# The images stage of a fused attention and expert kernel: VectorE's list reordered around the decay of scores, the scaling of the routed weights on ScalarE

## The reference

```python
h = h + attn(layernorm(h))      # scores = q @ k.T / sqrt(192) * 0.99 ** (i - j), causal, no softmax; scores @ v
h = h + moe(layernorm(h))       # 128 experts, the best 6 of each row, at most 192 rows an expert, plus a shared expert
```

```python
sig = sigmoid(x @ Wg.T)                       # 128 scores
topk_idx = top_k(sig + e_bias, 6)
topk_w = take_along_axis(sig, topk_idx)
topk_w = topk_w / (topk_w.sum(-1, keepdims=True) + 1e-20) * 2.5
```

## Time and profile before

| | us |
|---|---|
| median of 3 runs (762.48 to 763.86) | 762.79 |
| the profiled execution | 761.95 |
| its span, first to last instruction | 760.3 |
| PE busy | 685.0 (90%) |
| DVE busy | 480.9 (63%) |
| ACT busy | 318.4 (42%) |
| POOL busy | 200.9 (26%) |

### The profile page before, as it was taken

How to read it: one execution, slowest core, us unless ns; L and a number is a source line. 1 busy time by engine, 2 the same in 40 slices (tenths; PEclk the granted TensorE clock), 3 DMA queues, 4 the chain that set the end, 5 groups by cost and what they waited for, 6 DMA issues and landing times.

```text
span 760.3 us, 16584 instructions
## 1 busy us (share of the span) xinstructions
PE 685.0 (90%) x4587; PEld 639.9 (84%) x4588; DVE 480.9 (63%) x1534; ACT 318.4 (42%) x752; POOL 200.9 (26%) x312
## 2 busy tenths in 40 slices
PE   4799998999999847798999999999999999999993
PEld 4688888888888736687999999999999999999983
DVE  2257887788878864455566666757575657666641
ACT  1234544554455423244444443544344544453431
POOL 2113223222322200111123334333333323232330
PEclk9699999999999976899999999999999999999997
DMA  7127344633443232403145354545464645454531
GB/s 249 44 76 221 104 124 138 193 108 106 149 141 118 67 118 65 115 18 67 29 92 104 91 106 96 105 101 108 99 125 98 116 99 114 93 107 90 106 56 16
DMA packets 74005, 79.36 MB, mean 104 GB/s; under 512 B 6346, under 2 KB 65690, under 8 KB 73979
## 3 DMA queue, kind: packets, MB, share of 16 engines
q1 hardware_dynamic: 61482, 65.66, 30.6%
q0 software_dynamic: 12208, 12.75, 11.3%
q10 hardware_dynamic: 288, 0.66, 0.3%
HBM read 51.73 MB, written 19.32 MB: 93 GB/s over the span
## 4 chain that ended last, share of the span: by engine, by line
PE 45%; DMA 2%; DVE 2%; issue 2%; ACT 1%; DVEq 0%; POOL 0%; POOLq 0%; ACTq 0%
PE bank L1307 19%; PE bank L1277 9%; PE bank L1289 6%; PE bank L1322 6%; PE bank L1323 3%; DMA result<-y_rows,put_idx 2%; DVE s_inter L1521 1%; PE bank L1251 1%; PE bank L1326 1%; DVE s_rows L1536 1%; ACT s_rows L1171 0%; DVE y_rows L1508 0%; DVEq L998 0%; POOL result L1106 0%; DVE s_last L1529 0%
## 5 line engine op out<-in xcount | busy, mean ns | idle before, releaser
L1521 DVE TENSOR_TENSOR s_inter<-s_gate,bank 128x384 f32<-128x384 f32 (+1 forms) x112 | 60.4, 540 | 82.9 <-PE bank L1307 54.7
L1151 ACT ACTIVATE s_gate<-bank 128x384 f32<-128x384 f32 (+1 forms) x112 | 53.6, 479 | 93.9 <-PE bank L1307 89.0
L1322 PE MATMUL bank<-s_dn,s_in_hi 128*128 128x384 f32 (+1 forms) x287 | 88.7, 370 | 4.2 <-DVE s_rows L1536 3.0
L558 PE MATMUL bank<-w_tok,patches 128*128 128x192 f32 x384 | 72.6, 342 | 6.9 <-DMA patches<-xp 6.9
L1307 PE MATMUL bank<-all_hiA,s_hi 128*128 (+4 forms) x210 | 74.9, 357 | 3.7 <-DVE y_rows L1508 1.6
L1323 PE MATMUL bank<-s_dn,s_in_lo 128*128 128x192 f32 (+1 forms) x287 | 72.7, 253 | 0.0
L466 ACT ACTIVATE y<-h,shift,rstd 128x192 f32<-128x192 f32 (+2 forms) x96 | 45.6, 538 | 63.5 <-POOL shift L388 62.4
L558 PEld LDWEIGHTS bank<-w_tok,patches 128*128 128x128 f32 x384 | 65.8, 200 | 6.6 <-issue 6.5
L1099 POOL DMA_INDIRECT result<-y_rows,put_idx x40 | 60.6, 1514 | 39.9 <-DVE y_rows L1508 23.4
L1307 PE MATMUL bank<-all_B,s_hi 128*128 (+4 forms) x210 | 71.1, 338 | 0.0
L1307 PE MATMUL bank<-all_loA,s_hi 128*128 (+4 forms) x210 | 71.0, 338 | 0.0
(11 more groups left out here) (203 smaller groups left out, 1831.8 us busy)
## 6 DMA issues: line engine op xcount, KB each, us to landing
raw_gu<-wgu SPq DMA_DIRECT2D x22, 464.0 KB, 5.3
raw_gu<-wgu SPq DMA_DIRECT2D x44, 232.0 KB, 6.0
patches<-xp SPq DMA_DIRECT2D x16, 588.0 KB, 4.5
down_w<-wdn SPq DMA_DIRECT2D x22, 348.0 KB
result<-s_rows POOLq DMA_DIRECT2D x13, 288.0 KB
result<-h SPq DMA_DIRECT2D x16, 192.0 KB
yw_rows<-y SPq DMA_DIRECT2D x16, 192.0 KB
all_hiA<-y_hiA SPq DMA_DIRECT2D x16, 162.5 KB, 2.6
```

The costliest lines, as they stand in the source:

```text
L558: mm = pe.matmul(tok_ps[:, t * D:(t + 1) * D], patches[:, c, t * 128:(t + 1) * 128], w_tok[:, c, :], start=c == 0, stop=c == KC - 1)
L1151: act.activation(s_gate[m % 2][0:r, 0:width], up_banks(m, alone)[0][0:r, 0:width], ACT.Silu).then_inc(s_gate_ready, 1)
L1322: pe.matmul(bank[0:r, 0:2 * D], s_in_hi[:, m, rows], s_dn[:, m, :], start=m == 0, stop=False)
L1521: dve.tensor_tensor(s_inter[m % 2][0:r, 0:width], s_gate[m % 2][0:r, 0:width], up, ALU.mult).then_inc(s_inter_ready, 1)
```

## The change

On DVE `weights` is cut in two. `chosen_weights` (the three products with their sums) moves behind `decay` and `count_full`; `weight_sums` (the addition, into which a multiplication by 1/2.5 is put, and the reciprocal) moves behind `split_lo`. `split_lo` now stands ahead of `shared`. The three scalings leave DVE and become three ACT instructions, `weights(n-1)` on ACT, between `normed(n1, n+2)` and `sigmoid(n)`; the factor 2.5 is in the reciprocal. DVE has new waits for `w_ready` before it overwrites `w_raw` and `w_inv`. After the last image the order is `choose`, `count_full`, `chosen_weights`, `weight_sums`, and on ACT `counts`, `weights`. The other engines' lists are the same, and so is what is computed.

```diff
--- before.py
+++ after.py
@@ -480,6 +480,15 @@
                     act.activation(sig[:, 0:2, :], lg_ps[:, 0:2 * E].rearrange("p (t e) -> p t e", t=2), ACT.Sigmoid)
                     act.activation(sig[0:TL[2], 2, :], lg_ps[0:TL[2], 2 * E:3 * E], ACT.Sigmoid).then_inc(sig_ready, 1)
 
+                def weights(n):
+
+                    act.wait_ge(winv_ready, n + 1)
+                    wait(act, w_out, 32 * n)
+                    for t in range(3):
+                        r = TL[t]
+                        ins = act.activation(w_rows[0:r, t, :], w_raw[0:r, t, :], ACT.Identity, scale=w_inv[0:r, t:t + 1])
+                    ins.then_inc(w_ready, 1)
+
                 def counts(n):
                     act.wait_ge(ct_mm, n + 1)
                     wait(act, ct_ready, n)
@@ -504,6 +513,8 @@
                     split_hi(n)
                     if not isinstance(n, int) or n < B - 2:
                         normed(n1, h0[:, by_turns(n + 2), :], n + 2)
+                    if not isinstance(n, int) or n > 0:
+                        weights(n - 1)
                     sigmoid(n)
 
                 def shared_hi(half, i):
@@ -539,6 +550,7 @@
                 step(B - 2)
                 step(B - 1)
                 counts(B - 1)
+                weights(B - 1)
 
             @block.tensor
             def _(pe):
@@ -778,25 +790,23 @@
                     dve.tensor_tensor(chosen[0:TL[2], 2, :], left[0:TL[2], 2, 0:E], choice[0:TL[2], 2, 0:E],
                                       ALU.not_equal).then_inc(chosen_ready, 1)
 
-                def weights(n):
+                def chosen_weights(n):
 
                     dve.wait_ge(chosen_ready, n + 1)
+                    wait(dve, w_ready, n)
                     for t in range(3):
                         r = TL[t]
                         ins = dve.scalar_tensor_tensor(w_raw[0:r, t, :], sig[0:r, t, :], 1.0, chosen[0:r, t, :],
                                                        ALU.mult, ALU.mult, accum_out=w_sum[0:r, t:t + 1])
                         ins.then_inc(wraw_ready, 1)
+
+                def weight_sums(n):
                     dve.wait_ge(wraw_ready, 3 * n + 3)
-                    dve.tensor_scalar(w_sum2[:, :], w_sum[:, :], 1e-20, None, ALU.add).then_inc(wsum_ready, 1)
+                    dve.tensor_scalar(w_sum2[:, :], w_sum[:, :], 1e-20, 1.0 / SCALE, ALU.add,
+                                      ALU.mult).then_inc(wsum_ready, 1)
                     dve.wait_ge(wsum_ready, n + 1)
+                    wait(dve, w_ready, n)
                     dve.reciprocal(w_inv[:, :], w_sum2[:, :]).then_inc(winv_ready, 1)
-                    dve.wait_ge(winv_ready, n + 1)
-                    wait(dve, w_out, 32 * n)
-                    for t in range(3):
-                        r = TL[t]
-                        ins = dve.tensor_scalar(w_rows[0:r, t, :], w_raw[0:r, t, :], w_inv[0:r, t:t + 1], SCALE,
-                                                ALU.mult, ALU.mult)
-                    ins.then_inc(w_ready, 1)
 
                 def count_full(n):
 
@@ -816,17 +826,18 @@
                         choose(n - 1)
                     if more:
                         values(n + 1)
-                    if behind:
-                        weights(n - 1)
                     if ahead:
                         token_rows(n + 2)
                     if more:
                         decay(n + 1)
                     if behind:
                         count_full(n - 1)
+                        chosen_weights(n - 1)
+                    split_lo(n)
+                    if behind:
+                        weight_sums(n - 1)
                     if shared is not None:
                         shared()
-                    split_lo(n)
 
                 dve.wait_ge(pool_set, 2)
                 token_rows(0)
@@ -878,8 +889,9 @@
                 step(B - 2)
                 step(B - 1)
                 choose(B - 1)
-                weights(B - 1)
                 count_full(B - 1)
+                chosen_weights(B - 1)
+                weight_sums(B - 1)
 
 
 def block_b(nc, psum, all_hiA, all_loA, all_B, ident, ones, rest, iota, ecol, up_strict, images_full, countT,
```

## The result

| | before | after |
|---|---|---|
| median of 7 runs each, us | 762.72 (760.19 to 764.15) | 758.68 (756.44 to 761.27) |
| ratio to before | 1 | 0.9951 (95%: 0.9929 to 0.9973) |
| the profiled execution, us | 761.95 | 761.27 |

The change saves about 4.0 us, 0.5%. The profiled execution of after is the longest of its seven, so the same kernel was profiled once more as a control, and its columns stand beside it.

A forecast was written before the change was run, and what follows sets the result against it. PE was taken to be bound by its wait for DVE's late decay, about 1.1 us a round. Rounds -5.1 plus end 2.1 gave -3.0 us: 758.95 profiled, 759.8 as median; range 755.0 to 766.7.

The forecast's parts named there:

- the release of the decay: DVE, steps 1 to 13: with `weights` gone from ahead of `token_rows`, decay and attention product start 0.82 us earlier.
- if nothing else mattered: Plain round: the product of logits starts 0.71 us earlier, so a round would take 14.70 us in place of 15.41.
- `turned` follows `sigmoid` by 0.69: ACT, each round: start-to-start distance that put `turned` at 165.33, against 165.72 before.
- new wait of 0.3 at the query product: PE, each round: the query product starts only 0.39 us earlier, not 0.71; 13 x 0.39 = 5.1 us saved.
- rival A: ACT's new work is hidden: 13 x 0.71 = 9.2 us saved, less 2.1, giving 755.7 us; chance 0.14.
- The price of the scalings: ACT, each round: three scalings take 0.90 us, and the next instruction starts 0.81 after the first.
- Rival B: Scalings as slow as `normed`, 0.53 us more a round: 766.7 us, or 763.3 at half; chance 0.17 shared with another rival.
- The power stays slow: GpSimd's power keeps 1.32 us beside `chosen_weights`, not 0.88, as those products read two SBUF tensors each.
- SP's queue: Stores behind `w_ready`: `y2` issued 1.76 us after the first weights store, landing in 3.0; ACT waits 2 to 3.
- thin cover: PE's score product comes some 0.2 us late, taken in by its successor's wait for the decay; no charge.
- C's threshold of 4.55: Rival: SP's late `y2` store bounds rounds at 10.86 + landing, from 4.55 us landing; 768.2 to 775.9 us; chance 0.19.
- The end of the stage: After the last image nothing is hidden: last stores and the kernel's second half start 2.1 us later, charged in full.

The follow-up runs named there:

- the run that put loads ahead: Changed kernel with SP's six loads of the shared weights issued inside step 6, behind its patch and text loads: 756.92 us, 0.9927 of before.
- the run with `y2` last: Changed kernel with SP's two stores of `y2` moved behind the three stores of the normed operands: 771.23 us, 1.0141 of before.
- `y2` first: Changed kernel with SP's stores of `y2` and the normed operands ahead of its wait for the scaled weights: 756.28 us, 0.9912 of before.
- the best version: Changed kernel, `y2` and operand stores before SP's weights wait, `chosen_weights` and `weight_sums` before `count_full` after the last image: 750.82 us (0.9864), later 752.17 (0.9901).

## Why the prediction was right, and where it was not

759.8 was forecast, 758.68 measured; faster, inside the range. The total was right in part by luck: the rounds save 4.3 us more than forecast, and costs of 2.8 us were charged at nothing.

- **What bounds the kernel, and the release of the decay: right.** `token_rows` starts 0.48 us behind PE's counts (0.37 taken); DVE's wait there is 1.08 ("some 1"), PE's before the attention product 0.22 ("under 0.4"). The plain round is the 14.70 of "if nothing else mattered": 14.72.
- **The step that failed: "`turned` follows `sigmoid` by 0.69".** It follows by 0.42 (116.69, 117.11). The row of before that was taken, at 180.97, had a short wait for PE's transposes in it, too short to be bracketed: `sigmoid` was done at 180.82, the transposes only at 180.93.

```profile
180.49 0.44 PE L576 MATMUL bank<-ident,y 128*64 128x128 f32 x3
...
180.56 0.26 ACT L481 ACTIVATE sig<-bank 69x128 f32<-69x128 f32 x1
```

A distance between two starts is a duration only if the second waits for nothing. Add 0.12 less between `normed(n1)` and the scalings (1.33, not 1.45) and 0.06 at `normed(n1)`, less 0.07 more for the scalings, and `turned` is 0.38 earlier against the attention product than forecast. The new wait of 0.3 at the query product therefore is none, and 9.4 us are saved in the 13 rounds without the stall (199.86 - 191.14 + 0.68), not 5.1: that is rival A's round, though by a smaller chain and not by A's reason, as neither the power nor a scaling was at its lower end.
- **The price of the scalings: close.** 0.97 us for three (0.90), the next instruction after 0.88 (0.81). The estimate from the figures of the Trainium skill ("ScalarE: Activation LUTs", "What ACT_TABLE_LOAD costs") is 0.88, and the trace agrees. Rival B is out.
- **The power stays slow: right,** 1.26 for 1.32. The run that moved the two-input products off it gives 0.89. By the rule of the Trainium skill ("GPSIMD Engine Reference", Specifications) that is what should happen, and this run shows it.
- **SP's queue and "thin cover": right in a plain round.** `y2` goes out 1.77 us behind `w_rows` (1.76), lands in 2.9 (3.0); the score product is 0.16 late ("some 0.2") and the decay's wait takes it in. C's threshold of 4.55 was met once, in the run that put loads ahead; its sum is borne out part by part in the run with `y2` last (15.88 for 15.78).
- **Charged at nothing, wrongly.** The prediction listed what stands behind `w_ready` in SP's queue but stopped at the next residual's stores; behind those come, in one step, six loads and then the patches: 0.7 us in one execution, 3.6 in the other. And it took its cover from a plain round: step 14 has no patch product (+1.2 us, a wait of 0.3 and the clock at its lower level behind it), and step 15 waits for `y2` of image 14 (+0.9, which `y2` first takes away). What the clock makes of the 1.2 can be told from two executions of one other kernel, the best version with its scaling on VectorE: there this round took 13.59 us with the clock at 1.00 and 14.04 with it low, so some 0.45.
- **The end of the stage: right.** 2.2 to 2.3 us for 2.1.

In the control's trace: -9.4 + 0.7 + 1.2 + 0.9 + 2.2 = -4.4 us, against the -4.0 of the medians; in the profiled execution of after, whose stall cost 3.6, -1.3.

Reordering alone gives 0.9941, the scaling alone 0.9975, both 0.9945: as changed, the kernel gains nothing measurable from the scaling on ScalarE. In the traces, of the 2.2 us that it gains in the rounds (192.70 - 191.14, and the stall's 0.7) it gives back 1.3: at the stall, in the last round and on the way to the end; the 0.9 left is less than the medians can tell. With those mended it is worth 2.4 to 3.1 us.

## What to carry to other kernels

When a signal moves later, follow every queue that waits for it past its next step, to the loads that are issued only once, and redo the sum for the first and last steps, where the work that covers it is missing. Before two rows' distance is used as a cost, see that the second instruction was ready when the first ended. An engine that is idle for a fifth of each round can still have no room at the one place that matters: here, doubling the moved work showed the margin in one run.

## What the runs showed of the hardware

- The same patches, issued 3.35 us late in two executions of one kernel, cost PE 0.56 or 1.80 us of waiting. After the first its granted clock was 1.00 in the next 4 us, after the second 0.57, so that 1.8 us of idle time cost 3.6. The length of the idle time alone doesn't say when this happens: in step 14 the clock fell behind an idle time of 1.70 us in the control (0.66 and 0.50 in two windows), and stayed at 1.00 behind 1.40 in the kernel before and behind 1.71 with the scaling alone. In the best version with its scaling on VectorE it stayed at 1.00 behind 1.89 in one execution and fell behind the same 1.89 in the other (0.54 and 0.61).
- The two stores of `y2` (192 KB, and 52 KB behind it) released ACT 2.9 us after the issue of the first in a plain round, and 4.6 us after it with six loads issued 4 to 7 us ahead of it. With the same six issued 8 to 11 us ahead and the patches 6, in after, it was 3.8 (148.24 to 152.07).
- GpSimd's power on 128 x 3 took 0.88 or 0.89 us in step 1 and beside VectorE instructions with one operand in PSUM, and 1.26, 1.32 and 1.50 beside VectorE's two-input instructions in different orders.
